# A graph network on one core: preparation and first node stage in one section, and zeros issued without waits

## The reference

```python
# layer 0
msg = relu(concat([h[src], h[dst], w]) @ W1 + b1) @ W2 + b2
agg = where(deg > 0, segment_max(msg, dst), 0)
x = layernorm(x + relu(concat([h, agg]) @ U1 + c1) @ U2 + c2)
# layer 1: relu(concat([x[src], factors[dst]]) @ Wm + bm), summed by src ...
# layer 2: attention with 4 heads (softmax over the edges of a receiver)
# layer 3: two rounds of mean aggregation with W_in and W_out
```

## Time and profile before

| | us |
|---|---|
| median of 3 runs | 5741.72 (5738.06 to 5746.61) |
| profiled execution, own time | 5743.62 |
| its span | 5741.8 |
| preparation up to the indices (L612) | 252.8 |
| first scatter of node stage 0 (L748) | 268.5 |
| first gather of the first edge phase (L1108) | 357.5 |
| GpSimd busy, of the span | 3673.6 |

### The profile page before, as it was taken

The page is one execution under the profiler, slowest core; times in us unless marked ns, Lnnn a source line. Parts: engine busy times, 40 slices in busy tenths (PEclk is TensorE's granted clock), DMA queues, the critical chain, the costliest instruction groups (busy, mean ns, idle before and its releaser), DMA issues. The chain is left out here.

```text
span 5741.8 us, 88988 instructions
## 1 busy us (share of the span) xinstructions
PE 3292.9 (57%) x17957; PEld 2513.3 (44%) x17957; DVE 2408.0 (42%) x3908; ACT 1217.7 (21%) x2227; POOL 3673.6 (64%) x3810
## 2 busy tenths in 40 slices
PE   1268888888578886566666652333333443333335
PEld 0245555555356665456565652333333323333333
DVE  3323333333466665466666664222222222222224
ACT  0012222222234443122222221111111111111111
POOL 2277777777701004777777774777777767777776
PEclk7578999998799998678788875555555655555556
DMA  9969999998289996455555653444444444444443
GB/s 246 304 191 291 296 301 292 295 294 286 81 272 313 311 312 185 143 157 176 156 174 165 175 144 92 132 131 132 131 132 132 122 116 131 131 131 132 132 131 105
DMA packets 813159, 1087.16 MB, mean 189 GB/s; under 512 B 132097, under 2 KB 494202, under 8 KB 809690
## 3 DMA queue, kind: packets, MB, share of 16 engines
q1 hardware_dynamic: 371752, 390.56, 22.5%
q0 software_dynamic: 134688, 305.15, 21.1%
q10 hardware_dynamic: 306588, 390.09, 20.1%
HBM read 647.79 MB, written 437.96 MB: 189 GB/s over the span
## 5 line engine op out<-in xcount | busy, mean ns | idle before, releaser
L1108 POOL DMA_INDIRECT gath<-sender_table,src_cols x1664 | 1570.1, 944 | 576.3 <-issue 381.3
L1276 DVE TENSOR_TENSOR_SCAN scan<-meta,scan,bank 128x512 f32<-128x512 bf16 x624 | 798.6, 1280 | 1844.1 <-DVEq L1273 1833.9
L1163 PE MATMUL bank<-ident,gath 128*128 128x128 f32 x1664 | 464.0, 434 | 1276.1 <-DMA gath<-sender_table,src_cols 1276.1
L1466 POOL DMA_INDIRECT gath<-attention_table,src_cols x832 | 823.2, 989 | 262.9 <-issue 190.5
L1108 POOL DMA_INDIRECT gath<-joint_table,src_cols x832 | 813.3, 978 | 258.9 <-issue 188.7
L1163 PEld LDWEIGHTS bank<-ident,gath 128*128 128x128 f32 x1664 | 297.7, 217 | 1442.1 <-DMA gath<-sender_table,src_cols 1442.1
L1226 ACT ACTIVATE rows<-bank 128x512 f32<-128x512 f32 x624 | 372.6, 597 | 1995.4 <-ACTq L1224 1913.8
L1188 PE MATMUL bank<-ident,scan 128*128 128x128 f32 x2496 | 580.2, 379 | 4.8 <-PEq L1186 4.8
L1188 PEld LDWEIGHTS bank<-ident,scan 128*128 128x128 f32 x2496 | 478.9, 205 | 139.5 <-issue 139.5
L739 POOL DMA_INDIRECT gath<-scan_rows,end_i x147 | 140.9, 958 | 586.8 <-ACTq L1394 542.9
L1506 PE MATMUL bank<-recv,same 128*128 128x4 f32 x1664 | 225.5, 259 | 161.9 <-PEq L1504 161.6
(11 more groups left out here) (242 smaller groups left out, 5028.6 us busy)
## 6 DMA issues: line engine op xcount, KB each, us to landing
recv<-receiver_rows SPq DMA_DIRECT2D x624, 256.0 KB
scan_rows<-rows ACTq DMA_DIRECT2D x624, 256.0 KB
attention_scan_rows<-rows ACTq DMA_DIRECT2D x208, 264.0 KB
receiver_rows<-gath ACTq DMA_DIRECT2D x26, 2048.0 KB, 12.1
factor_rows<-gath ACTq DMA_DIRECT2D x208, 256.0 KB
gath<-factor_rows SPq DMA_DIRECT2D x208, 256.0 KB
scan_rows<-rows SPq DMA_DIRECT2D x208, 256.0 KB
meta<-edge_meta ACTq DMA_DIRECT2D x416, 128.0 KB
```

Source lines behind the costliest of these rows:

```text
L1108: pool.indirect_dma_start(out=landed[s][:, c, 0:width], out_offset=None, in_=table[:, :], in_offset=bass.IndirectOffsetOnAxis(ap=src_cols[ ...
L1163: ins = pe.transpose(b[:, c * P:(c + 1) * P], g[:, c, 0:F], ident[:, :])
L1276: chain(v.tensor_tensor_scan(scan[s % 2][:, :], go_on, src, scan[1 - s % 2][:, EB - 1:EB], ALU.add if expands else ALU.mult, ALU.max if ex ...
L1466: pool.indirect_dma_start(out=gath[s][:, c, :], out_offset=None, in_=att_d[:, :], in_offset=bass.IndirectOffsetOnAxis(ap=src_cols[:, t:t + ...
```

## The change

- The preparation arrays that lay in `x_nm` get space of their own, and the gathered receiver rows go into `bar_c` and `first_c` instead of `xT`. So x can be loaded during the preparation: SP issues it right behind `lasts`, ahead of the edge marks.
- Preparation and node stage 0 are one block. Each engine goes on into its part of node stage 0 when its own preparation is written out. SP hands out most tokens at its very start; PE waits for the weights and x; POOL waits until all 26 zero pieces have landed and the indices are ready.
- PE's two transposes of the start rows move from behind the factor work into step 5 of its node stage 0 (behind the tables of group 2 and the turn of group 3).
- ACT issues six zero pieces at once, then one behind each of the 13 factor loads, then the last seven, and waits for none of them.
- The counting goes in five parts of 12, 12, 12, 12 and 4 node tiles.
- In node stages 0 and 1 the copy to `recv_o` moves from DVE to ACT, as the first piece of ACT's step.
- In node stage 0 the mark loads go one to a step, from step 2 on, in front of that step's stores, and behind the clearing of `scan_rows`.

`node_phase` moves up in the file as a whole; the diff below leaves the move out.

```diff
-        agg, aggT, y_nm, prod = recv[0:2], scan, recv[2:4], [sb(f"prod{s}", [P, EB]) for s in range(2)]
+        agg, aggT, y_nm = recv[0:2], scan, recv[2:4]
 # node_phase, sync
+                def load_marks(q, s):
+                    g = 2 * q + s
+                    if g < 2 * HEADS:
+                        t, m = ((bar_c, 1), (first_c, 2))[g % 2]
+                        sp.dma_start(t[g // 2::HEADS, :, :], meta_d[m, :].rearrange("(b t e) -> t b e", t=RT, e=P)).then_inc(t_marks, 16)
+                    elif g == 2 * HEADS:
+                        sp.dma_start(last_bar[:, :], last_first_d[0, :].partition_broadcast(HEADS)).then_inc(t_marks, 16)
-                work = [(0, store_table)] * (to_d is not None) + ...
+                work = [(2, load_marks)] * (k == 0) + [(0, store_table)] * (to_d is not None) + ...
                 if k == 0:
-                    for h in range(HEADS):
-                        for t, m in ((bar_c, 1), (first_c, 2)):
-                            sp.dma_start(t[h::HEADS, :, :], meta_d[m, :].rearrange("(b t e) -> t b e", t=RT, e=P)).then_inc(t_marks, 16)
-                    sp.dma_start(last_bar[:, :], last_first_d[0, :].partition_broadcast(HEADS)).then_inc(t_marks, 16)
 # node_phase, vector
-                work = [(new + 3, receivers)] * makes_recv + ...
+                work = [(new + 3, receivers)] * (k == 2) + ...
 # node_phase, scalar
+                def receivers(q, s):
+                    w = GROUP_TILES[2 * q + s]
+                    if q > 0:
+                        act.wait_ge(n_recv_stored[s], 16)
+                        act.sem_inc(n_recv_stored[s], -16)
+                        act.wait_ge(scattered[s], q * (16 * CT) + 16 * tiles_of[s] * scattered_before)
+                    act.wait_ge(n_recv_ps, 1)
+                    act.sem_inc(n_recv_ps, -1)
+                    chain(act.activation(recv_o[s][:, 0:w, :], bank[recv_bank][:, 0:w * F].rearrange("p (t f) -> p t f", f=F), ACT.Copy))
+                    act.sem_inc(n_bank_free[recv_bank], 1)
+                    act.sem_inc(n_recv, 1)
+                    act.sem_inc(n_recv_sc, 1)
-                work = ([(new + 2, table)] * (w_tab is not None) + ...
+                work = ([(new + 3, receivers)] * (k in (0, 1)) + [(new + 2, table)] * (w_tab is not None) + ...
 # node_phase, tensor(pe, turn_starts=None)
+                def starts(q, s):
+                    if q == s == 0:
+                        turn_starts()
-                        + [(2, product_rows), (1, product), (0, turn_agg)] * dense)
+                        + [(2, product_rows), (1, product), (0, turn_agg)] * dense + [(5, starts)] * (k == 0))
 # preparation
-            dst_r, src_r = carve("x", [TC, P], I32), carve("x", [TC, P], I32)
+            dst_r, src_r = psb("dst_r", [P, TC, P], I32), psb("src_r", [P, TC, P], I32)
...
-            found = xT[:, :].rearrange("p (t k) -> p t k", k=P)
-            quarter = (0, 12, 26, 40, NT)
+            found = [t[:, :, :].rearrange("p b e -> p (b e)").bitcast(F32).rearrange("p (t k) -> p t k", k=P) for t in (bar_c, first_c)]
+            fifth = (0, 12, 24, 36, 48, NT)
 # sync
                     sp.dma_start(lasts[:, :], last_dst_d[0, :].partition_broadcast(P)).then_inc(lasts_in, 16)
+                    sp.wait_ge(n_load_ready, 1)
+                    sp.sem_inc(n_load_ready, -1)
+                    sp.dma_start(x_nm[:, 0:whole, :], a["x"][0:whole * P, :].rearrange("(t p) f -> p t f", p=P)).then_inc(n_load, 16)
+                    sp.dma_start(x_nm[0:N - whole * P, whole, :], a["x"][whole * P:N, :]).then_inc(n_load, 16)
...
                     sp.wait_ge(scores_ready, 1)
                     sp.sem_inc(scores_ready, -1)
-                    sp.wait_ge(weights_in, 16 * 18)
-                    (the load of x, and the wait for it)
-                    (the tokens)
+                    sync_first(sp)
 # scalar
+                    def fill(lo, hi):
+                        for j in range(lo, hi):
+                            act.dma_start(z[:, j:j + 1, :], zeros.unsqueeze(1)).then_inc(zeroed, 16)
+                    def fill_one(q, s):
+                        fill(6 + q * SLOTS + s, 7 + q * SLOTS + s)
+                    fill(0, 6)
-                    steps(act, NG, SLOTS, (0, load), (0, fill), (3, keep_turned), (4, store))
-                    act.wait_ge(zeroed, 32)
-                    act.sem_inc(zeroed, -32)
+                    straight(NG, SLOTS, (0, load), (0, fill_one), (3, keep_turned), (4, store))
+                    fill(6 + NG, 2 * NG)
...
+                    for free in (n_x_bank_free, n_bank_free[7], n_bank_free[5]):
+                        act.sem_inc(free, 1)
+                    scalar_first(act)
 # gpsimd
+                    pool.wait_ge(zeroed, 32 * NG)
+                    pool.sem_inc(zeroed, -32 * NG)
+                    pool.wait_ge(index_ready, 1)
+                    pool.sem_inc(index_ready, -1)
+                    gpsimd_first(pool)
 # vector, at its end
+                    v.sem_inc(index_ready, 1)
+                    vector_first(v)
 # tensor
                     steps(pe, NG, SLOTS, (0, turn), (1, product))
-                    (the two transposes of the start rows)
+                    def turn_starts():
+                        (the two transposes of the start rows)
+                    pe.wait_ge(weights_in, 16 * 18)
+                    pe.wait_ge(n_load, 32)
+                    tensor_first(pe, turn_starts)
...
-        run(node_phase(0))
```

More of the change, by code:

```diff
@@ new lines, in gnn_program @@
+        t_gathered = [sem(f"t_gathered{s}") for s in range(2 * STRETCH)]
+        t_er = sem("t_er")
+        t_em = sem("t_em")
+        t_last = sem("t_last")
+        t_carry = sem("t_carry")
+        t_dlast = sem("t_dlast")
+        t_dcarry = sem("t_dcarry")
+        t_sum = sem("t_sum")
+        t_weighted = sem("t_weighted")
+        t_scoreT = sem("t_scoreT")
+        t_lastT = sem("t_lastT")
+        t_carryT = sem("t_carryT")
+        t_dlastT = sem("t_dlastT")
+        t_dcarryT = sem("t_dcarryT")
@@ L1086, in edge_phase @@
+        t_sumT = sem("t_sumT")
+        t_below = sem("t_below")
+        t_exp_v = sem("t_exp_v")
+        t_exp_p = sem("t_exp_p")
+        t_added = sem("t_added")
         def edge_phase(k):
```

782 lines of the change are left out of this document (374 added, 408 removed).

## The result

The changed kernel takes 5802.2 us (median of 4 runs, 5800.8 to 5804.9), the kernel before 5740.3 (4 runs); the ratio is 1.0107, 95% interval 1.0095 to 1.0119. Forecast was 5716, so the change is slower by 62 us where I had it faster by 26. The profiled executions differ by 57.9 us of span (5799.7 against the earlier trace rows).

What follows compares the result with a forecast made beforehand. It took the preparation to run beside a saturated DMA and the node stage to be paced by POOL's issue. +8 (`start_f`), -35.6 (to the third group) and +1.5 (after it) made -26 us: 5716, range 5692 to 5742.

Steps and rivals of the forecast that it cites:

- The change reaches only its first 358 us and one copy later on: Scope of the forecast: only the head and the copy in node stage 1 could change, the latter by 0 us.
- `loaded` at 50.5: Head: first loads land at 50.5 us instead of 35.9, +15 us, behind six zero pieces queued at once.
- One for one: Beside zeros, SP's queue q1 moves one small packet for each 16 KB packet of q10, 27 a us.
- The empty spell of q10: Head: q10 without packets from 63 to about 73 us, letting SP's small transfers catch up at 520 a us.
- `start_f` at 236.5: End of the five-part counting: `start_f` made at 236.5 us against 228.5, +8; bounds -10 and +35.
- PE stands ready at its step 5, so the transpose no longer waits: After the counting: the start rows' copy begins 2.2 us behind `start_f` instead of 12.1.
- The zeros have ended (224 against 251): Before the first scatter: the last zero pieces have landed near 224 us, so they hold nothing up.
- -25.1: Stretch from `start_f` to the first scatter: 14.9 us instead of 40.0.
- The stall before the third group: Node stage 0: POOL's wait before the third group's scatter shrinks from 11.2 us to 1.
- The marks among the stores: Node stage 0: mark loads share q1 with stores, 4.9 of 5.1 us a step; +1.5 for the stretch, bounds 0 and +10.
- the gain is eaten: Rival, chance 0.14: delay of 23 to 45 us at `start_f` from the head cancels the gain, 5731 to 5752 us.
- "one for one" at full (5791): Rival, chance 0.12: queues alternate packets throughout, delaying row loads and gathers, +83 us at `start_f`; +49, 5791 us in all.

Runs made afterwards that it cites:

- b1: The kernel before with 102 do-nothing instructions on VectorE, its attention loop at 2227 (51 past a multiple of 128): 5812.4 us, ratio 1.0117.
- h3: The changed kernel with 154 do-nothing instructions on VectorE and the turn of the row starts as first piece of TensorE's node stage: 5770.9 us, ratio 1.0035.
- a1: The changed kernel with 154 do-nothing instructions on VectorE, its attention loop back at 2125 (77 past a multiple of 128): 5769.1 us, ratio 1.0041.
- h5: The changed kernel with 154 do-nothing VectorE instructions, zeros paced by waits, row starts turned between TensorE's factor steps: 5765.7 us, ratio 1.0030.
- a3: The changed kernel with 40 do-nothing instructions on VectorE, its attention loop at 2011 (91 past a multiple of 128): 5742.1 us, ratio 0.9993.
- h8: The changed kernel with 40 VectorE fillers, leading zero pieces moved to factor steps 4 to 9, row starts turned first in node stage: 5754.4 us, ratio 1.0006.

## Why the prediction was wrong

- **"The change reaches only its first 358 us and one copy later on".** This is the step that failed, with 56 of the 58 us. I had counted the copy that moved to ScalarE as time (right: node stage 1 lost nothing, 1440.2 to 1438.9 for its first gather) and not as instructions that leave a stream. b1 prices it with nothing else changed: +65 us. With it gone the changed kernel stands at 1.0041 (77 past) or 0.9993 (91 past), so the rest of the forecast is to be judged by the head.
- **`loaded` at 50.5.** It came at 65.3. One for one needs packets of q1 that can flow; SyncE's issue was held (24.6 us for one transfer, 25.9 for seven), so q1 got 60 to 88 packets in 8 us and not 218. The empty spell of q10 was forecast (63 to 73; it lasted to 85) and gave back half of the 29 us. `lasts` landed at about 98 (first count at 98.27), +12.5 instead of +7.
- **`start_f` at 236.5.** 239.0, in the range. The first part of rows cost a wait of 22.5 us where about 12 was taken.
- **"PE stands ready at its step 5, so the transpose no longer waits".** This is the step that failed in the head: 18.3 us from `start_f` to the turn. ScalarE ended its factor steps at 231 and not near 190, because zeros blocked its issue, and TensorE's steps in front of the turn wait for ScalarE. h3 against a1 shows that the order on TensorE is the cause (2.1 us from `start_f` to its copy instead of 16.9), and so does h5.
- **"The zeros have ended (224 against 251)".** They ran to about 269, and the store of the row starts went behind them: 12.7 us instead of 4.2. Of the -25.1 for this stretch nothing came: `start_f` to first scatter took 40.6 us (40.0 before).
- **The stall before the third group.** Right: it is gone, 11 us. **The marks among the stores.** Right, no gap. The block's end cost 4.3 us more than before, which I had at nothing. So the 30 us between -26 and +4 are 2.5 at `start_f`, 25.7 from there to the first scatter and 4.3 at the block's end, less some 2 at the scatters.
- The rival "the gain is eaten" (0.14) had the size of the head, +4 us in place of -26, but not its mechanism: it wanted 23 to 45 us of delay at `start_f`, which came 10.5 late. That untouched code could lose 56 us stood nowhere; 5802 lies above every rival, "one for one" at full (5791) included, and that one's delays weren't there.

## What to carry to other kernels

When an edit moves instructions from one engine to another, or adds or removes some, look where each long loop behind it lies in its engine's stream: idle stretches marked "issue" at one place of each turn, and more packets on the instruction queue, are its sign, and a few fillers that do nothing, in time that is idle anyway, are both test and cure. A large transfer that nothing waits for isn't free: here it held the issue of its own engine (166 us in place of 40) and, in the first 65 us, that of SyncE, so put it behind the first loads. A short step that a chain waits for belongs in front of the long steps of its engine; taking it there shows the next bound, so price the chain and not the step. And profile a head more than once before reading a few us from it.

## What the runs showed of the hardware

- A loop of 307 instructions on VectorE took some 6 us more a turn at 51 past a multiple of 128 in the stream than at 77 past (88.7 us in b1, 82.6 in the kernel before, in the mean of ten turns), with 49 to 52 packets of 8 KB more on the instruction queue over ten jumps back.
- Without any refetching the place still moved the phase: 1067 us at 91 past and 1083 to 1090 at 77 past in the changed kernel's family, by longer gather instructions of GpSimd (980 ns in the mean in a3, 1004 in a1).
- The issue of one unpaced piece of 2 MB held ScalarE for 31 us (h8), and SyncE's issue of one transfer of 62 rows took 24.6 us beside such pieces (1.6 in the kernel before).
